# Weighted sums of an attention stage in query ranges of up to 512 instead of 256

## The reference, cut to what matters

```python
# x: (1, 1024, 512); H = 32 heads of HD = 16, G = 8 key/value groups, REP = 4 heads per group
scores = einsum('bhqd,bhkd->bhqk', q, k)            # causal: -inf where key > query
weights = softmax(scores * (1.0 / HD ** 0.5), axis=-1)
ctx = einsum('bhqk,bhkd->bhqd', weights, v)
```

## Time and profile before

| | us |
|---|---|
| median of three runs | 951.99 |
| the profiled execution | 950.2 |
| its span, first to last instruction | 948.2 |
| attention steps of group 4 (one of the loop) | 305.31 to 343.31 |
| attention steps of group 6 | 380.57 to 409.15 |
| PE busy over the span | 749.5 (79%) |
| DVE busy | 601.0 (63%) |
| ACT busy | 342.7 (36%) |

### The profile page before, as it was taken

One profiled execution on the slowest core, in us unless ns is written; L12 is line 12 of the kernel. 1 busy time (PEld: TensorE's weight loads), 2 busy tenths in 40 slices (PEclk: granted clock), 3 DMA queues, 4 the chain that ended last, 5 costly groups with the idle time before them and its releaser, 6 DMA issues.

```text
span 948.2 us, 14477 instructions
## 1 busy us (share of the span) xinstructions
PE 749.5 (79%) x4054; PEld 305.2 (32%) x4054; DVE 601.0 (63%) x1455; ACT 342.7 (36%) x551; POOL 273.0 (29%) x248
## 2 busy tenths in 40 slices
PE   1957765889889898988749989998322799999993
PEld 1622221222223222223314434353121445444441
DVE  7513865777676776502699899966999855931004
ACT  1112224556555565773003232357113233222220
POOL 3023443112212122122105544545102044323331
PEclk9977756999989999999879999998766799999997
DMA  9499899833022221451223655320599220021001
GB/s 260 80 142 320 241 236 226 167 78 64 27 47 55 42 46 37 107 114 36 56 45 87 206 178 77 75 91 0 139 191 210 56 45 1 5 39 45 1 0 44
DMA packets 144216, 92.84 MB, mean 98 GB/s; under 512 B 111720, under 2 KB 123112, under 8 KB 143960
## 3 DMA queue, kind: packets, MB, share of 16 engines
q1 hardware_dynamic: 133120, 69.93, 33.6%
q10 hardware_dynamic: 10816, 16.91, 6.0%
q0 software_dynamic: 240, 5.51, 2.8%
HBM read 48.20 MB, written 29.04 MB: 81 GB/s over the span
## 4 chain that ended last, share of the span: by engine, by line
PE 52%; DVE 18%; DMA 10%; issue 6%; SPq 6%; ACT 4%; POOL 3%; DVEq 0%; ACTq 0%; POOLq 0%
PE ps L1126 19%; PE ps L1138 9%; PE ps L1402 8%; PE ps L1370 7%; PE ps L1379 5%; DVE mx L1286 3%; DMA lora_d<-arena 2%; DMA lorad_d<-arena 2%; SPq L345 2%; PE ps L1111 2%; DMA qp_d<-arena 1%; POOL arena L975 1%; DVE arena L1282 1%; DVE stats L468 1%; ACT arena L1349 1%
## 5 line engine op out<-in xcount | busy, mean ns | idle before, releaser
L1126 PE MATMUL ps<-arena 128*128 128x512 f16 (+1 forms) x976 | 223.3, 386 | 18.3 <-DMA arena<-arena 18.0
L1349 ACT ACTIVATE arena<-ps 128x1024 f32<-128x1024 f32 (+7 forms) x256 | 163.6, 652 | 116.0 <-PE ps L1379 111.2
L1370 PE MATMUL ps<-arena 96*128 (+4 forms) x384 | 135.0, 377 | 36.9 <-DVE mx L1286 16.0
L1282 DVE CUSTOM_DVE_ANT_0 arena<-ps,arena 128x256 bf16<-128x256 f32 (+3 forms) x256 | 122.0, 489 | 58.8 <-PE ps L1370 51.0
L970 POOL TENSOR_TENSOR arena<-arena (+2 forms) x50 | 70.6, 1412 | 253.5 <-ACT arena L902 247.2
L1126 PEld LDWEIGHTS ps<-arena 128*128 (+2 forms) x976 | 97.0, 100 | 138.2 <-issue 30.4
L1379 PE MATMUL ps<-arena 99*128 (+4 forms) x384 | 125.6, 344 | 4.7 <-ACT arena L1349 4.4
L1138 PE MATMUL ps<-arena 128*128 (+3 forms) x488 | 117.6, 391 | 14.1 <-POOL arena L975 13.9
L1257 POOL TENSOR_SCALAR_AFFINE_SELECT arena<-arena 128x512 f32<-128x512 f32 x64 | 40.9, 640 | 224.9 <-ACT arena L1349 224.7
L1286 DVE TENSOR_REDUCE mx<-ps 128x1 f32<-128x512 f32 x128 | 88.2, 689 | 27.4 <-PE ps L1370 26.5
L1402 PE MATMUL ps<-arena 128*32 128x256 f32 (+1 forms) x1280 | 100.3, 387 | 2.8 <-POOL arena L1257 2.3
(11 more groups left out here) (154 smaller groups left out, 761.8 us busy)
## 6 DMA issues: line engine op xcount, KB each, us to landing
arena<-qp_d SPq DMA_DIRECT2D x48, 128.0 KB, 4.7
lora_d<-arena ACTq DMA_DIRECT2D x20, 256.0 KB, 4.5
arena<-lora_d SPq DMA_DIRECT2D x10, 512.0 KB, 4.3
w1n_d<-arena SPq DMA_DIRECT2D x10, 512.0 KB, 3.2
arena<-rec_d SPq DMA_DIRECT2D x32, 128.0 KB, 2.6
qp_d<-arena SPq DMA_DIRECT2D x12, 256.0 KB, 4.7
w1dn_d<-arena SPq DMA_DIRECT2D x4, 704.0 KB, 3.2
arena<-in_L_ffn_down_w_dram ACTq DMA_DIRECT2D x16, 172.0 KB, 3.5
```

The source lines that it names most:

```text
L1126: last = nc.tensor.matmul(ps[0:h, 2 * (n % 2) + o, :], w(t[0])[:, kt, bass.ds(ht * P, h)], xt[:, c, t[1], kt, :], start=(kt, t) == (0, ter ...
L1282: nc.vector.tensor_tensor_reduce(out=junk[:, h, 0:w], in0=s_bank(g, u)[:, 0:w], in1=strip[:, D - w:D], scale=1.0, scalar=3.0 * NEG, op0=AL ...
L1349: nc.scalar.activation(probs[:, kt % 2, h, kt * P:T], st_bank(h).rearrange("p b n -> p (b n)")[:, kt * P:T], ACT.Exp, scale=HD ** -0.5).th ...
L1370: nc.tensor.matmul(s_bank(g, u)[:, 0:k1 - k0], qt6[0:QROWS, g % RING, h, qt * P:(qt + 1) * P], kt6[0:QROWS, g, k0:k1], start=True, stop=Tr ...
```

## The change

Ranges are 512 queries wide where the causal limit allows, aligned to 512, and the slots are listed anew.

```diff
         def row_ranges(kt):

-            return [(max(q, kt * P), q + 2 * P) for q in range(T - 2 * P, kt * P - 2 * P, -2 * P)]
+            return [(max(q, kt * P), q + 4 * P) for q in range(T - 4 * P, kt * P - 4 * P, -4 * P)]
...
-        SUM_SLOTS = ((2,), (3, 4, 6, 7), (3, 4, 6, 7), (3, 5, 7), (1, 2, 3), (2, 3), (2, 3), (2,))
+        SUM_SLOTS = ((2,), (4, 6), (4, 6), (4, 6), (1, 3), (2,), (2,), (2,))
```

## The result

The changed kernel takes 971.97 us (median of four runs, 967.92 to 974.44) against 952.86 for the kernel before beside it: a ratio of 1.0205, 95% interval 1.0152 to 1.0258. The forecast was 965, the range 948 to 975. The profiled execution took 974.44 us, the slowest of the four; the one of before took 950.2.

The account below looks back on a forecast made before the run. PE looks like the bound, but outside step 4 it waits for DVE or ACT. Six groups at 1.4 (8.4) plus 5.2 gives 13.6 us on 950.2: 963.8; the median lies 1.8 higher: 965, range 948 to 975.

Parts of the forecast that it names:

- The wide range: On PE, a range of 512 takes 1.00 us, extended from widths 128 and 256; bounds 0.85 and 1.16.
- The 0.24 per removed range: On PE, each range's fixed cost with entry; 64 ranges removed, 15.4 us of PE work.
- Step 1 and the wait behind it: Slot 7 of step 1 starts 0.57 us late, moving PE's release in step 2; that wait exceeds 2.2 us, was 1.70.
- Step 2 at full clock: Step 3 starts +0.7 us late at full clock, +0.32 at group 4's half clock.
- Reciprocals: End of step 2: no range covers DVE's last maxima and reciprocals; group 4's delay goes from +0.32 to +0.83 us.
- the walk: Slot-by-slot timing of PE's matmuls and waits after the change, through group 4: about +1.4 us at the group's end.
- Step 3's slots: Pairs of slots at 1.25, 1.71 and 1.25 us; group 4's delay goes from +0.83 to +1.22 us.
- Steps 4 to 7: Step 4 waits +0.24 for an exponential, savings in steps 5 and 6 become waiting; group ends about +1.4 us.
- Groups 6 and 7: PE waits for ACT where ranges stood, and for a mask in step 6: 2.7 and 2.5 us, together 5.2.
- The slots together: All eight groups: 8.4 us for six groups plus 5.2 for groups 6 and 7, 13.6 us slower.
- a rival with 9%: More half clock after longer PE waits: one more stretch in each of seven groups, 12 us, 977 us; chance 0.09.
- The first rival, the saving that comes through,: PE sets the pace in steps 1 to 6, idle time unchanged: all 15.4 us saved, 937 us; chance 0.13.

Follow-up runs that it names:

- the back-to-back run: Old ranges of 256 at the changed kernel's places, two behind one slot where it has one wide range; 966.51 us, ratio 1.0157 to the kernel before.
- the pair with step 2 filled: Changed kernel and kernel before, each issuing slot 1's transposed score matmul in step 2 eight times in six groups; 961.76 and 944.28 us.
- the doubly filled pair: Changed kernel and kernel before, each with seven extra matmuls in step 2 and eight narrow ones ending step 7, in six groups; 959.72 and 939.46 us.
- the early part alone: Kernel before with only steps 1 and 2 as in the changed kernel (wide ranges behind slots 4 and 6); 956.15 us, ratio 1.0059.
- late part alone: Kernel before with only steps 3 to 7 as in the changed kernel, steps 1 and 2 as before; 962.24 us, ratio 1.0132.

## Why the prediction was right, and where its sizes were off

**Direction and mechanism.** The forecast said that PE's queue looks like the bound and is not, that the saved 15.4 us turn into waits, and that more comes on top. The runs show this: other slots for the same ranges take the loss away, the same slots with narrow ranges keep it, and at equal mean clock it is still there.

**The wide range.** Taken as 1.00 us from two widths; measured 1.00. The 0.24 per removed range holds by the distance of the starts, since each of them stood alone between matmuls of the full array; the back-to-back run corrects what it is: the price of entering and leaving, not of the range. The profile's busy time of PE does not fall by the forecast 1.9 in a group, only by 0.77 at full clock (33.86 to 33.09 in the pair with step 2 filled); why I did not trace.

**Step 1 and the wait behind it.** Forecast: slot 7 is 0.57 late, and with it the release of slot 2 in step 2. Counted from the start of step 1: slot 7 at 326.11 - 320.31 = 5.80 us against 316.07 - 310.85 = 5.22, and the release at 329.69 - 320.31 = 9.38 against 319.66 - 310.85 = 8.81. Late by 0.58 and 0.57. The wait was to be over 2.2 us in one piece; it is 2.20 in two.

**Step 2 at full clock.** Forecast +0.7 from the start of step 1 to that of step 3. From the doubly filled pair, step 1 is 6.39 against 6.50 and step 2 7.75 to 7.92 against 7.14: 0.5 to 0.67.

**Reciprocals.** Forecast 0.5 late; measured 0.3 (step 3 of the early part alone). From slot 7 of step 2 to slot 2 of step 3 the walk has 2.11 us (325.62 to 327.73); in group 3 of the early part it is 1.89 (288.61 to 290.50). The walk set the last maxima and the reciprocals end to end (0.42, where the reciprocals follow after 0.35: 289.11 to 289.46), rounded 326.81 up to 326.9, and took 0.83 from the next maxima to slot 2 where it is 0.77 (289.73 to 290.50). **Step 3's slots**: forecast 0.39 (1.22 less 0.83), measured 0.32 (late part alone).

**Steps 4 to 7.** Forecast +0.18 (1.22 to 1.4 in the walk); measured +0.42, from 12.34 to 12.76. Step 4 loses 0.23 where the walk had it level, steps 5 and 6 save 0.27, and step 7 takes 3.31 us where it took 2.85: with no range behind slot 3 of step 6 it starts sooner and its slot 1 waits for the last maxima of step 6. The walk had this wait; its sum for the four steps was short by a quarter of a microsecond. Over a full group the terms at full clock come to 1.5 to 1.7 us, and so do the groups of the filled pair; forecast 1.4.

**Groups 6 and 7.** Forecast +2.7 and +2.5; group 6 measured +2.61, group 7 +3.5 with more of it at half clock. Group 6 had 0.9 us at half clock in its last step; wholly at full clock (the changed kernel with step 2 filled) it takes 30.78 us, +2.2. The waits are where the walk has them: PE stands for ACT in steps 2, 3, 4 and 6, up to 0.69 us at a time, and for the mask in steps 6 and 7.

**The slots together.** Forecast 13.6; measured 15.4 at equal mean clock. That the two are so near is partly luck, and that the figure is that of the removed PE work as well is chance. Groups 0 to 5 cost 12.3 us (232.8 against 220.5) where the forecast has 8.4, two half-clock stretches included; groups 6 and 7 cost 3.1 (61.5 against 58.5) where it has 5.2. The sum itself is 965.5 to 965.6, not 965, by its own terms: 963.8 + 1.8, with +1.3 for group 0 in place of 1.4.

**The clock.** The median, 971.97, is 7 us over the forecast. The sum counted the half-clock time as unchanged, and put more of it into a rival with 9%. In the profiled execution it did come: in groups 1 to 5 the wait of step 2 is followed by 3.4 us (twice) or 6.8 us (three times) at half clock, before the change by 3.4 each time, and step 0 runs at half clock in three of these groups where it was one. What is left of the stage's 24.0 us after 15.4 for the slots is 8.6, where that rival said 12. TensorE's clock has two levels and falls after idle time, as the Trainium skill says (TensorE: Matmul & The Clock Gate, What's actually happening). The stretches at 1.00 and 0.50 above agree; here the clock fell though PE had been busy for 1.21 of the 3.40 us before. The forecast's mechanism and this rival were not alternatives: in this execution the longer wait is followed by more half clock. Whether that makes the 7 us of the median is not shown, since the fillings, which take most of the stretches away, leave the distance of the medians at 20.3 us. The errors of the slots' terms alone (15.4 for 13.6) are 1.8 of the 7.

**The first rival, the saving that comes through,** falls with PE's idle time in the attention: 284.06 - 253.92 = 30.1 us before, 308.10 - 260.99 = 47.1 after.

**The split between the steps.** The prediction put the loss mostly into steps 1 to 3. By the parts run alone, steps 3 to 7 cost more than steps 1 and 2 (1.32% against 0.59%). In a full group at full clock the order is still that of the walk, 0.8 to 1.0 us (step 2 and the reciprocals) against 0.74; what turns it over lies outside of these: groups 6 and 7 (1.5 and 2.4 us more than before in the late part's profile) and half clock in step 0 (7.1 to 7.5 us in four of its six groups, 5.5 at full clock) are in the late part. The early part's median is only 4.9 us over before, less than its full-clock terms and its last two groups make together in the profile; that is open.

## What to carry to other kernels

Where PE and another engine turn in a two-buffer loop (here 1.25 us per pair of slots, with PE work in it or without), a piece of work that fits into the loop's idle time (here 0.57 us) is free, and merging it away or moving it gains nothing; merged with another into 1.00 us it is no longer free (step 3: 5.50 us for 5.10). What counts is what covers the last wait ahead of a serial piece on another engine: keep one piece there, and merge only pieces that are neighbours or stand where PE alone is busy. If a wait must remain, look for half clock behind it: here 3.4 or 6.8 us of it followed.

## What the runs showed of the hardware that was not expected

- Repeating matmuls to no purpose made the program faster. Seven of them (1.5 us of PE time) in each of six waits of about 2 us took 8.7 us off the kernel before (952.97 to 944.28), and with eight narrow ones at the end of the groups 13.7 (953.13 to 939.46, ratio 0.9807). In the profiles of both the half-clock stretches in step 2 were gone. With the first filling alone others had come in step 0 (40.4 us at half clock in the attention against 30.6), with both 19.9 were left.
- Four fp32 matmuls on the four column groups run side by side: their eight records of 0.6 us each all start within 0.5 us, and 512 columns of four heads take 1.00 us, of which 0.15 is fixed by the prediction's line, and the entry costs 0.09 more. The fixed part is shared by ranges back to back.
- The same code ahead of the attention took from 146.2 to 154.0 us in the twelve profiles. Nothing in any edit touches it. One profile against one profile can't tell 5 us of the whole; the stage alone is better, but its half-clock stretches also differ from execution to execution.
